# Graph network with four residual layers, one core: two rows per block on GpSimd, attention's closing steps moved behind the next block's masked scores, and the layer steps placed 8 groups later

## The chip, the cores and the metric

The kernel runs on one core of one Trainium2 chip. The metric is device time in microseconds (us). The core's engines are TensorE (PE in the profile; PEld is its weight load), VectorE (DVE), ScalarE (ACT), GpSimd (POOL) and SyncE (SP, which issues all DMAs here). They run side by side and wait for each other only at semaphores that the kernel writes out.

## The reference, cut to what matters

```python
x = LN(x + graph_conv(x, adj, L0_W, L0_b))      # layer 0: D^-1/2 (A+I) D^-1/2 x W^T + b
x = LN(x + attention(x, adj, WQ, WK, p))        # layer 1
x = LN(x + graph_conv(x, adj, L2_W, L2_b))      # layer 2
x = LN(x + graph_conv(x, adj, L3_W, L3_b))      # layer 3: D^-1/2 A D^-1/2 x W + b
# attention, for x of 8 x 2048 x 128, adj of 8 x 2048 x 2048:
q = x @ WQ;  k = x @ WK
h = relu(q[:, None, :, :] + k[:, :, None, :])   # 8 x 2048 x 2048 x 128
score = einsum('bijd,d->bij', h, p)
att = softmax(score + where(adj > 0, 0, -1e22)) ; out = att @ x
```

The tensor `h` is never stored. For each pair of sample and node i ("a row") the kernel makes a 128 x 2048 tile (feature by j) and TensorE contracts it with p at once.

## The kernel before, in words

**Blocks, groups, rows.** A sample has 16 blocks of 128 nodes, 128 blocks in all. A block has 32 groups (`g` 0 to 31) of 4 rows (`u` 0 to 3); "(1,3)" is row 3 of group 1. Twelve groups are of kind A (2, 5, 7, 10, 13, 15, 18, 21, 23, 26, 29, 31): ScalarE makes their rows, L861. The 20 others are of kind D: VectorE makes them as `max(q, -k)` on pairs of fp16, L1110. TensorE takes the groups in order, L1269. Each kind has a ring of 2 groups: the rows of a D group may only be made when TensorE has finished the D group before the last one (semaphore `rows_used["D"]`). Group 3 uses the slot of group 0, group 6 that of group 3, and so on.

**The order is written out by hand.** Each engine walks over `place = t*32 + g` and does at a place whatever the tables at the top of `build` put there, before or between the rows of that group. "Place 28" below is the group before whose rows the work stands.

**Masked scores.** The scores of block n are read out of PSUM inside block n+1 at (1,1): `masked_scores` (L1048, L1052). Its four bank reads wait for TensorE's last groups of block n (`bank_scored`, `rows_used`), and TensorE's group 0 of block n+1 waits bank by bank for them (`scores_read`). ScalarE takes the exponentials at place 5, TensorE turns them and multiplies by x at places 6 to 23, and VectorE ends the attention of block n at place 27 (`norm_inputs`: L1056, L1060, L1063, L1066: division by the row sum, residual, statistics) and place 30 (`att_out`, L1070). POOL computes the inverse root in between (`att_root`, L668, L670).

**Rows on other engines.** POOL makes row (1,3) of nearly every block (`row`, L679); it waits for the first bank of masked scores to be read. In 84 blocks it also makes row (30,3) (`sum_row`, L691), while VectorE does a layer step's sum; in the same number of cases VectorE makes a row of kind A (L1090).

**Layer steps beside the attention.** While attention runs on one sample, layers 2 and 3 of the sample before it and layer 0 of the one after it run in 12 steps of 512 nodes: layer 2 from blocks 2 to 5, layer 3 from 6 to 9, layer 0 from 10 to 13. A step adds 16 adjacency pieces (`add_piece`, L1183, at `PIECES_AT`), the self loop (`add_self`, L1189), is copied by ScalarE (`turn_layer`, L793), projected (`project`, L1201), summed with statistics by VectorE (`sum_layer`, L976, L984, L990) and normalised (`norm_layer`, L997); its bias is `add_bias`, L966. Layer 0 is followed by the new queries and keys (`QK`; L1213 and `split`, L1010, L1016). The first sample has no layers 2 and 3, the last has no layer 0. In blocks 0 to 9 also the next sample's adjacency is turned (`turn_unit`, places 0, 6, 10, 14, 18, 23, 28) and summed on ScalarE.

## Time and profile before

| | us |
|---|---|
| median of 3 runs | 13880.72 (13879.03 to 13884.08) |
| profiled execution, span | 13883.0 (no other time of it is given; it lies within the runs) |
| busy in it: DVE / PE / ACT / POOL | 13327.1 / 12956.7 / 12942.7 / 1095.3 |
| granted TensorE clock, mean | 0.989 |

The span runs from the first to the last instruction. Some 188 us at the start (first sample's adjacency) and 177 us after the last masked scores have no attention rows beside them; between them lie 127 intervals of 98 to 109 us, one per block. Idle time counts only where the engine is waited for afterwards, so what matters is the stretch of a block in which each engine waits.

### The profile page before, as it was taken

The numbers are of one execution on the slowest core, as the hardware profiler recorded it, in microseconds if no ns is written. First come the engines' busy times: TensorE is split into PE (matmuls) and PEld (weight loads), VectorE is DVE, ScalarE is ACT, GpSimd is POOL, SyncE is SP. The second block draws the span as 40 slices with busy tenths as digits, with TensorE's granted clock in tenths as the row PEclk, the third lists the DMA queues.
The fourth block names the chain that finished last, engine by engine and source line by source line (L and its number), as shares of the span: only waits on it lengthen the run. The fifth ranks groups of instructions, "written<-read, shape, count | busy, mean of one in ns | idle before, by whom it ended". The sixth has DMA issues, their size and how long they took to land.

```text
span 13883.0 us, 318102 instructions
## 1 busy us (share of the span) xinstructions
PE 12956.7 (93%) x143877; PEld 5442.7 (39%) x143877; DVE 13327.1 (96%) x14041; ACT 12942.7 (93%) x8528; POOL 1095.3 (8%) x706
## 2 busy tenths in 40 slices
PE   7889989999899999999999998999989999899988
PEld 3333434443344333444334443344434444333333
DVE  7999999999999999999999999999999999999995
ACT  6999999999999999999999999999999999999994
POOL 0000000010000100010000100001100010000000
PEclk9999999999999999999999999999999999999999
DMA  4111112221122112221122211222112221011103
GB/s 144 52 46 49 50 58 84 89 63 44 61 90 90 59 37 74 86 87 56 44 72 86 84 59 37 77 87 84 59 36 82 84 80 58 32 49 52 43 12 111
DMA packets 680284, 918.70 MB, mean 66 GB/s; under 512 B 60432, under 2 KB 421904, under 8 KB 659472
## 3 DMA queue, kind: packets, MB, share of 16 engines
q1 hardware_dynamic: 678928, 898.35, 20.7%
q8 instruction: 1129, 18.50, 0.6%
q14 instruction: 227, 1.86, 0.0%
HBM read 705.23 MB, written 184.55 MB: 64 GB/s over the span
## 4 chain that ended last, share of the span: by engine, by line
DVE 56%; PE 34%; ACT 7%; issue 2%; DMA 1%; POOL 0%; SPq 0%; DVEq 0%; POOLq 0%; ACTq 0%
DVE big L1110 50%; PE score L1269 24%; ACT big L861 6%; PE acc L1183 5%; PE acc L1242 2%; PE turn L1154 2%; DVE att L1048 2%; DVE big L1090 1%; DVE gx L997 1%; DMA piece<-adj_turned 0%; DVE gx L976 0%; PE turn L1213 0%; DVE stats L984 0%; ACT q_pair L769 0%; DVE att L1037 0%
## 5 line engine op out<-in xcount | busy, mean ns | idle before, releaser
L1110 DVE TENSOR_SCALAR big<-q_pair,k_pair_cols 128x2048 f32<-128x2048 f32 x10029 | 12094.2, 1278 | 289.8 <-PE score L1269 272.4
L861 ACT ACTIVATE big<-q_f,k_cols 128x2048 f32<-128x2048 f32 x6060 | 11633.5, 1998 | 256.9 <-PE score L1269 247.5
L1269 PE MATMUL score<-big,unit_window 128*32 128x512 f16 x82592 | 5439.0, 394 | 750.3 <-DVE big L1110 716.7
L1269 PE MATMUL score<-big,sign_window 128*32 128x512 f32 x48480 | 5591.5, 595 | 69.2 <-ACT big L861 67.5
L1269 PEld LDWEIGHTS score<-big,unit_window 128*32 128x32 bf16 x82592 | 2308.1, 96 | 3952.0 <-DVE big L1110 1128.8
L1269 PEld LDWEIGHTS score<-big,sign_window 128*32 128x32 f32 x48480 | 1572.3, 110 | 3299.2 <-issue 2948.4
L1183 PE MATMUL acc<-piece,q_f 128*128 128x512 f32 x2944 | 1411.5, 602 | 18.1 <-DVE q_f L959 10.7
L668 POOL TENSOR_SCALAR att_var<-att_mom 128x1 f32<-128x1 f32 x128 | 73.4, 573 | 9809.0 <-DVE att_mom L1066 9809.0
L1183 PEld LDWEIGHTS acc<-piece,q_f 128*128 128x128 f32 x2944 | 503.1, 190 | 529.8 <-issue 470.2
L1242 PE MATMUL acc<-x,att_turned 128*128 128x128 f32 x4096 | 559.4, 280 | 0.0
L1242 PEld LDWEIGHTS acc<-x,att_turned 128*128 128x128 f32 x4096 | 504.1, 194 | 56.8 <-issue 56.8
L837 ACT ACTIVATE att_turned<-turn 128x512 f32<-128x512 f32 x512 | 299.6, 585 | 160.1 <-PE turn L1154 160.0
L769 ACT ACTIVATE q_pair<-turn 128x512 f32<-128x512 f32 x448 | 261.4, 584 | 146.7 <-PE turn L1154 146.6
L679 POOL TENSOR_SCALAR big<-q_pair,k_pair_cols 128x2048 f32<-128x2048 f32 x127 | 250.5, 1973 | 1436.5 <-DVE bank_max L1048 1436.5
L1154 PEld LDWEIGHTS turn<-ident,att 128*128 128x128 f32 x2048 | 220.3, 143 | 340.8 <-issue 335.8
L1154 PE MATMUL turn<-ident,att 128*128 128x128 f32 x2048 | 343.6, 291 | 3.8 <-ACT att L833 3.1
L1048 DVE CUSTOM_DVE_ANT_0 att<-score,att 128x512 f32<-128x512 f32 x512 | 323.1, 684 | 10.4 <-PE score L1269 10.3
L1154 PE MATMUL turn<-ident,q_pair 128*128 128x128 f32 x1920 | 296.7, 279 | 27.3 <-DMA q_pair<-in_adj_dram 20.3
L833 ACT ACTIVATE att<-att,neg_max 128x2048 f32<-128x2048 f32 x128 | 256.1, 2000 | 51.5 <-DVE neg_max L1052 51.5
L1154 PEld LDWEIGHTS turn<-ident,q_pair 128*128 128x128 f32 x1920 | 219.6, 142 | 122.8 <-issue 92.9
L691 POOL TENSOR_SCALAR big<-q_pair,k_pair_cols 128x2048 f32<-128x2048 f32 x84 | 165.6, 1971 | 1110.2 <-DVE gx L976 1110.2
L782 ACT ACTIVATE y_turned<-q_pair 128x1024 bf16<-128x1024 f32 x224 | 237.1, 1059 | 7.1
(95 smaller groups left out, 2876.3 us busy)
## 6 DMA issues: line engine op xcount, KB each, us to landing
piece<-adj_turned SPq DMA_DIRECT2D x1472, 256.0 KB, 2.7
att<-in_adj_dram SPq DMA_DIRECT2D x128, 1024.0 KB, 5.2
q_pair<-in_adj_dram SPq DMA_DIRECT2D x240, 512.0 KB, 4.5
adj_turned<-q_pair SPq DMA_DIRECT2D x224, 512.0 KB, 4.8
adj_turned<-big SPq DMA_DIRECT2D x16, 1024.0 KB, 13.5
q_f<-in_adj_dram SPq DMA_DIRECT2D x16, 512.0 KB, 5.4
gx<-in_x_dram SPq DMA_DIRECT2D x32, 256.0 KB, 4.0
q_kept<-q_pair SPq DMA_DIRECT2D x32, 256.0 KB, 3.7
```

The costliest lines, as they stand in the source:

```text
L679: pool.tensor_scalar(ring["D"][:, RANK[g] % RING * 4 + u, :], pairs_of(c + 1), 3.0e38, k_pair_cols[:, t % 2, QUAD * u + g:QUAD * u + g + 1 ...
L769: nc.scalar.activation(stage(c)[:, k * BANK:(k + 1) * BANK], turn[1][:], ACT.Copy).then_inc(turn_free[1], 1)
L782: nc.scalar.activation(unread, raw(c), ACT.Abs, accum_out=abs_part[:, u % 2, u // 2:u // 2 + 1]).then_inc(raw_abs_summed, 1)
L833: nc.scalar.activation(att[:], att[:], ACT.Exp, bias=neg_max[:], accum_out=row_sum[:]).then_inc(exp_ready, 1)
L837: nc.scalar.activation(att_turned[:, cc % 2, :], turn[0][:], ACT.Copy).then_inc(turn_free[0], 1)
L861: ins = nc.scalar.activation(ring["A"][:, RANK[g] % RING * 4 + u, :], q_of(c + 1), ACT.Relu, bias=k_cols[:, t % 2, QUAD * u + g:QUAD * u + ...
L1048: nc.vector.tensor_tensor_reduce(out=part, in0=score[:, cc, :], in1=part, scale=1.0, scalar=-3.0e38, op0=ALU.add, op1=ALU.max, accum_out=b ...
L1110: ins = nc.vector.tensor_scalar(ring["D"][:, RANK[g] % RING * 4 + u, :], pairs_of(c + 1), k_pair_cols[:, t % 2, QUAD * u + g:QUAD * u + g ...
L1154: ins = nc.tensor.transpose(turn[k][:, j * P:(j + 1) * P], src(j), ident[:])
L1183: nc.tensor.matmul(acc[1][:], scaled(c)[:, i, :], turned, start=(i == 0), stop=(i == T - 1)) \
L1242: ins = nc.tensor.matmul(acc[0][:, 0:D], att_turned[:, cc % 2, j * P:(j + 1) * P], x1[:, cc * PER + j, :], start=(cc == 0 and j == 0), sto ...
L1269: ins = nc.tensor.matmul(score[QUAD * u:QUAD * (u + 1), cc, :], (unit_window if pair else sign_window)[:, QUAD - 1 - g:2 * QUAD - 1 - g], ...
```

## The change

POOL makes (3,3) as well as (1,3), both right after VectorE has made row (1,0) (new semaphore `window_open`). `norm_inputs` of block n goes from place 27 of block n+1 to right behind the masked scores in block n+2, `att_out` to place 6 there; `row_sum` gets two columns since the next exponentials come before it is read. All layer steps start 8 groups later (`STEP_SHIFT`), and the tables within a step are set anew.

```diff
+    BLOCK, STEP_SHIFT = {"layer2": 2, "layer3": 6, "layer0": 10}, 8
-    PIECES_AT = {-4: [0, 1, 2], 0: [3, 4, 5], 1: [6], 4: [7], 10: [8, 9], 14: [10], 18: [11], 23: [12, 13, 14, 15]}
-    SELF_AT, TURNED_AT, PROJECT_AT, SUM_AT, ROOT_AT, NORM_OUT_AT, STORE_AT = 18, 28, 28, 31, 33, 40, 41
+    PIECES_AT = {-4: [0, 1], 0: [2], 2: [3], 6: [4], 10: [5], 15: [6, 7, 8], 20: [9, 10, 11], 24: [12, 13, 14], 25: [15]}
+    SELF_AT, TURNED_AT, PROJECT_AT, SUM_AT, ROOT_AT, NORM_OUT_AT, STORE_AT = 15, 28, 28, 31, 33, 37, 38
...
-    QK = {"turn": 46, "copy": 49, "q": 50, "q_out": 54, "k": 55, "q_store": 56, "q_split": 58, "k_out": 59,
+    QK = {"turn": 47, "copy": 50, "q": 52, "q_out": 55, "k": 56, "q_store": 57, "q_split": 59, "k_out": 60,
...
+        row_sum = sb("row_sum", [P, 2])
...
-        MASK_AT, EXP_AT, NORM_AT, OUTPUT_AT = 24, 5, 27, 30
+        MASK_AT, EXP_AT, OUTPUT_AT = 24, 5, 6
-        POOL_ROW = (1, 3)
+        POOL_ROWS = [(1, 3), (3, 3)]
-        SUM_ROW = (30, 3)
+        SUM_ROW = ((SUM_AT + STEP_SHIFT - 1) % GROUPS, 3)
...
         def start_of(name, s):
-            return (BLOCK[name] + s) * GROUPS
+            return (BLOCK[name] + s) * GROUPS + STEP_SHIFT
...
-            def row(c, t):
-                g, u = POOL_ROW
+            def row(c, t, g, u):
                 n = block_of(c, t)
-                pool.wait_ge(scores_read, block_of(c, t) * CHUNKS + 1)
+                pool.wait_ge(window_open, n)
...
                 pool.wait_ge(rows_used["D"], n * N_OF["D"] + (RANK[g] + 1))
...
-                    if g == POOL_ROW[0] and has_pool_row(c, t):
-                        row(c, t)
+                    if g == POOL_ROWS[0][0] and has_pool_row(c, t):
+                        for at in POOL_ROWS:
+                            row(c, t, *at)
+                        if has_norm(c, t):
+                            att_root(block_of(c, t) - 2)
...
-                    if before and g == NORM_AT:
-                        norm_inputs(c * T + (T + t - 1), c + 1 if t > 0 else c, (t - 1) % T)
-                    if before and g == OUTPUT_AT:
-                        att_out(c * T + (T + t - 1), (t - 1) % T)
+                    if has_norm(c, t) and g == OUTPUT_AT:
+                        att_out(n - 2)
...
                             if before and u > 0 and (g, u) == masked_at(t):
                                 masked_scores(n)
+                                if has_norm(c, t):
+                                    norm_inputs(n - 2)
-                            if (g, u) == POOL_ROW and has_pool_row(c, t):
+                            if (g, u) in POOL_ROWS and has_pool_row(c, t):
                                 continue
...
+                            if before and (g, u + 1) == masked_at(t):
+                                ins.then_inc(window_open, 1)
```

Modulo 32, the pieces stood at places 28, 0, 1, 4, 10, 14, 18, 23 (3, 3, 1, 1, 2, 1, 1, 4 of them) and now stand at 28, 0, 1, 4, 8, 10, 14, 18, 23 (3, 3, 1, 2, 1, 1, 1, 1, 3). Projection goes from place 28 to 4 of the next block, the sum from 31 to 7, the normalisation from 8 to 13, the bias from 20 to 28, the self loop from 18 to 23.

VectorE, in a block in which layer 3 runs, before: from the statistics of the attention (`att_mom`) over a layer step's sum (L976 to L990) and the masked scores to the step's normalisation (L997).

```order
L1066 BN_AGGR att_mom<-att_stats 128x2
L1110 TENSOR_SCALAR big<-q_pair,k_pair_cols 128x2048 x8
L1070 TENSOR_SCALAR att_pre<-att_pre,att_mom,att_rstd 128x128
L1110 TENSOR_SCALAR big<-q_pair,k_pair_cols 128x2048 x3
L976 SCALAR_TENSOR_TENSOR gx<-acc,dis_use,gx 128x128 x4
L984 BN_STATS stats<-gx 128x6 x4
L990 BN_AGGR moments<-stats 128x2 x4
L1110 TENSOR_SCALAR big<-q_pair,k_pair_cols 128x2048 x5
```

The same engine in the same block now, from the last masked read on.

```order
L1062 TENSOR_REDUCE neg_max<-bank_max 128x1
L1067 RECIPROCAL row_inv<-row_sum 128x1
L1071 SCALAR_TENSOR_TENSOR att_pre<-acc,row_inv,x 128x128
L1074 BN_STATS att_stats<-att_pre 128x6
L1077 BN_AGGR att_mom<-att_stats 128x2
L1120 TENSOR_SCALAR big<-q_pair,k_pair_cols 128x2048 x9
L1082 TENSOR_SCALAR att_pre<-att_pre,att_mom,att_rstd 128x128
L1120 TENSOR_SCALAR big<-q_pair,k_pair_cols 128x2048 x3
L986 SCALAR_TENSOR_TENSOR gx<-acc,dis_use,gx 128x128 x4
L994 BN_STATS stats<-gx 128x6 x4
L1000 BN_AGGR moments<-stats 128x2 x4
L1120 TENSOR_SCALAR big<-q_pair,k_pair_cols 128x2048 x16
```

Attention's statistics and the step's sum stood before the masked scores and stand behind them; of the 14 rows that VectorE made from (1,1) to the end of group 6 it makes 12, the other two being POOL's (3,3) and (6,3), the row beside the sum.

TensorE at places 28 and 4, before: first place 28 with the projection (L1201) and three pieces, then place 4 with one piece.

```order
L1154 MATMUL turn<-ident,q_pair 128x128 x4
L1201 MATMUL acc<-w_layer,y_turned 128x128 x4
L1183 MATMUL acc<-piece,q_f_0 128x512 x3
L1269 MATMUL score<-big,unit_window 32x512 x32
...
L1183 MATMUL acc<-piece,q_f_0 128x512
L1269 MATMUL score<-big,unit_window 32x512 x32
L1269 MATMUL score<-big,sign_window 32x512 x16
```

TensorE at the same two places now.

```order
L1167 MATMUL turn<-ident,q_pair 128x128 x4
L1196 MATMUL acc<-piece,q_f_0 128x512 x3
L1282 MATMUL score<-big,unit_window 32x512 x32
...
L1214 MATMUL acc<-w_layer,y_turned 128x128 x4
L1196 MATMUL acc<-piece,q_f_0 128x512 x2
L1282 MATMUL score<-big,unit_window 32x512 x32
L1282 MATMUL score<-big,sign_window 32x512 x16
```

The projection has left place 28 and stands at place 4, with one more piece behind it.

## Rows read from the trace of the kernel before

**Rows 1.** The page: busy us (share of span) by engine; the chain by engine

```profile
PE 12956.7 (93%) x143877; PEld 5442.7 (39%) x143877; DVE 13327.1 (96%) x14041; ACT 12942.7 (93%) x8528; POOL 1095.3 (8%) x706
DVE 56%; PE 34%; ACT 7%; issue 2%; DMA 1%; POOL 0%; SPq 0%; DVEq 0%; POOLq 0%; ACTq 0%
```

**Rows 2.** Waits over the span: us in total, times, longest

```profile
PE score L1269 <- DVE big L1110: 716.7, 577, 2.8
DVE big L1110 <- PE score L1269: 272.4, 305, 2.7
```

**Rows 3.** Windows from masked score to masked score: blocks 0, 7, 12; PE, PEld, DVE, ACT, POOL

```profile
5258.34:5361.49 103.15, 91.84 (x1103) 38.12 (x1102) 101.83 (x98) 100.01 (x74) 5.41 (x3) 0.98 0.17 54
6003.53:6110.54 107.01, 103.76 (x1141) 44.32 (x1142) 103.63 (x113) 105.04 (x75) 8.34 (x6) 1.00 0.32 96
6538.54:6645.62 107.08, 103.70 (x1129) 43.13 (x1128) 104.69 (x116) 99.05 (x61) 9.91 (x6) 1.00 0.21 62
```

**Rows 4.** Timeline, DVE, blocks 6 to 7: start, us, what, [idle before]

```profile
5979.47 0.15 DVE L1056 RECIPROCAL row_inv<-row_sum 128x1 f32<-128x1 f32 x1
...
5980.38 0.18 DVE L1066 BATCH_NORM_AGGREGATE att_mom<-att_stats 128x2 f32<-128x6 f32 x1
5981.78 9.65 DVE L1110 TENSOR_SCALAR big<-q_pair,k_pair_cols 128x2048 f32<-128x2048 f32 x8 [1.22 <-PE score L1269]
...
5995.19 1.12 DVE L976 SCALAR_TENSOR_TENSOR gx<-acc,dis_use,gx 128x128 f32<-128x128 f32 x4
...
5997.55 6.04 DVE L1110 TENSOR_SCALAR big<-q_pair,k_pair_cols 128x2048 f32<-128x2048 f32 x5
6003.51 0.68 DVE L1048 CUSTOM_DVE_ANT_0 att<-score,att 128x512 f32<-128x512 f32 x1
...
6006.14 16.93 DVE L1110 TENSOR_SCALAR big<-q_pair,k_pair_cols 128x2048 f32<-128x2048 f32 x14
6022.98 1.11 DVE L997 TENSOR_SCALAR gx<-gx,moments,rstd 128x128 f32<-128x128 f32 x4
...
6044.80 2.48 DVE L1110 TENSOR_SCALAR big<-q_pair,k_pair_cols 128x2048 f32<-128x2048 f32 x2 [1.56 <-PE score L1269]
```

**Rows 5.** Timeline, PE, block 7: groups 31, 0 and 9

```profile
6000.72 2.76 PE L1269 MATMUL score<-big,sign_window 128*32 128x512 f32 x24
...
6006.57 2.00 PE L1269 MATMUL score<-big,unit_window 128*32 128x512 f16 x32
...
6033.72 2.01 PE L1269 MATMUL score<-big,unit_window 128*32 128x512 f16 x32 [1.73 <-DVE big L1110]
```

**Rows 6.** Timeline, PE, block 0: group 0

```profile
5259.16 2.38 PE L1269 MATMUL score<-big,unit_window 128*32 128x512 f16 x32 [0.43 <-DVE bank_max L1048]
```

**Rows 7.** Timeline, POOL: a row and a small operation, block 7; two small ones elsewhere

```profile
6004.30 1.97 POOL L679 TENSOR_SCALAR big<-q_pair,k_pair_cols 128x2048 f32<-128x2048 f32 x1 [6.68 <-DVE bank_max L1048]
6006.23 1.27 POOL L662 TENSOR_SCALAR var_eps<-moments 128x4 f32<-128x4 f32 x1
...
4710.19 0.23 POOL L668 TENSOR_SCALAR att_var<-att_mom 128x1 f32<-128x1 f32 x1 [76.86 <-DVE att_mom L1066]
...
6239.47 11.93 POOL L704 TENSOR_TENSOR dis_new<-deg_sum,minus_half 128x16 f32<-128x16 f32 x3 [15.31 <-DVE deg_sum L942]
```

**Rows 8.** Timeline, DVE beside the last of rows 7

```profile
6239.31 14.44 DVE L1110 TENSOR_SCALAR big<-q_pair,k_pair_cols 128x2048 f32<-128x2048 f32 x12
```

**Rows 9.** Groups by line: shape xcount | busy us, mean ns | idle before

```profile
L1183 PE MATMUL acc<-piece,q_f 128*128 128x512 f32 x2944 | 1411.5, 602 | 18.1 <-DVE q_f L959 10.7 <-DMA piece<-adj_turned 6.3
...
L1201 PE MATMUL acc<-w_layer,y_turned 128*128 128x128 f32 x768 | 106.9, 282 | 8.9 <-ACT y_turned L793 8.9
...
L966 DVE TENSOR_TENSOR gx<-gx,bias_layer 128x512 f32<-128x512 f32 x96 | 65.5, 682 | 0.1
```

**Rows 10.** Timeline, ACT, block 7: exponentials; the wait at place 13

```profile
6007.84 1.99 ACT L833 ACTIVATE att<-att,neg_max 128x2048 f32<-128x2048 f32 x1
...
6037.68 0.60 ACT L769 ACTIVATE q_pair<-turn 128x512 f32<-128x512 f32 x1 [1.81 <-PE turn L1154]
```

More of the change, by code:

```diff
@@ L273, in pool_rows, with pool_rows_before, has_norm @@
         def pool_rows(c, t):
-            return max(c * T + (T + t - 1), 0)
-        SUM_ROW = (30, 3)
+            return max(c * T + (T + t - 1), 0) * len(POOL_ROWS)
+        def pool_rows_before(g):
+            return sum(h < g for h, _ in POOL_ROWS)
+        def has_norm(c, t):
+            return block_of(c, t) > 1
+        SUM_ROW = ((SUM_AT + STEP_SHIFT - 1) % GROUPS, 3)
         def sums_at(c, t):
-            return steps_at(c, t * GROUPS + SUM_AT, SUM_AT)
+            return steps_at(c, t * GROUPS + SUM_ROW[0] + 1, SUM_AT)
         def has_sum_row(c, t):
@@ L294, in lent_rows @@
                 return []
-            return LENT_ROWS[:1 if steps_at(c, t * GROUPS + SELF_AT, SELF_AT) else 2]
+            return LENT_ROWS[:1 if steps_at(c, t * GROUPS + STEP_SHIFT, 0) else 2]
         def lent_before(c, t, g):
@@ L617, in attention @@
                             load_q(c + 1)
-                    if before and g == OUTPUT_AT + 1:
-                        store_x2(c * T + (T + t - 1), (t - 1) % 2)
+                    if block_of(c, t) > 1 and g == OUTPUT_AT + 1:
+                        store_x2(block_of(c, t) - 2, t % 2)
             sp.dma_start(diag[:], diagonals[0], allow_slow_non_contiguous=True).then_inc(diag_loaded, 16)
@@ L642, in _ @@
             attention(LAST)
-            store_x2(B * T - 1, 1)
+            for m in (B * T - 2, B * T - 1):
+                store_x2(m, m % 2)
             for place in range(PLACES):
@@ L737, in _ @@
             attention(LAST)
-            att_root(B * T - 1)
+            for m in (B * T - 2, B * T - 1):
+                att_root(m)
             for place in range(PLACES):
@@ L832, in exponentials @@
                 act.wait_ge(neg_max_ready, n)
-                nc.scalar.activation(att[:], att[:], ACT.Exp, bias=neg_max[:], accum_out=row_sum[:]).then_inc(exp_ready, 1)
+                nc.scalar.activation(att[:], att[:], ACT.Exp, bias=neg_max[:],
+                                 accum_out=row_sum[:, (n - 1) % 2:(n - 1) % 2 + 1]).then_inc(exp_ready, 1)
             def copy_weights(m, cc):
@@ L1066, in norm_inputs, with att_out @@
                 nc.vector.bn_aggr(att_mom[:], att_stats[:]).then_inc(att_moments_ready, 1)
-            def att_out(m, t):
+            def att_out(m):
+                t = m % T
                 dve.wait_ge(att_rstd_ready, m + 1)
@@ L1084, in attention @@
                     side(c, place)
-                    if before and (g, 0) == masked_at(t):
-                        masked_scores(n)
                     for h, u in lent_rows(c, t):
@@ L1123, in _ @@
             masked_scores(B * T)
-            norm_inputs(B * T - 1, B - 1, T - 1)
-            att_out(B * T - 1, T - 1)
+            for m in (B * T - 2, B * T - 1):
+                norm_inputs(m)
+                att_out(m)
             for place in range(PLACES):
@@ L1248, in score_rows @@
                 kind, n = KIND[g], block_of(c, t)
-                if g == POOL_ROW[0] and has_pool_row(c, t):
-                    pe.wait_ge(pool_row_ready, pool_rows(c, t) + 1)
+                if g in [h for h, _ in POOL_ROWS] and has_pool_row(c, t):
+                    pe.wait_ge(pool_row_ready, pool_rows(c, t) + pool_rows_before(g) + 1)
                 if g == SUM_ROW[0] and has_sum_row(c, t):
```

16 lines of the change are left out of this document (7 added, 9 removed).

## The prediction

> **What bounds the kernel now.** Read the page first: three engines are busy for 93 to 96% of the span, and the chain goes through VectorE for 56% and TensorE for 34% [rows 1]. No engine bounds it alone. The waits say the same: TensorE waits 716.7 us for VectorE's rows, VectorE 272.4 us for TensorE [rows 2]. So it matters where in a block each wait falls, and the windows show that this depends on the kind of block [rows 3]. In block 0, without a layer step, VectorE is busy 101.83 of 103.15 us and TensorE 91.84: VectorE bounds it. In block 7, with a step, idle are TensorE 3.2 us, VectorE 3.4 and ScalarE 2.0; in block 12 3.4, 2.4 and 8.
>
> The timeline of block 7 gives the places. M is the start of its masked scores (6003.51). VectorE waits 1.22 us for TensorE ahead of place 27 (5981.78), then not until place 14, where it waits 1.56 (6044.80) [rows 4]. TensorE waits 1.73 us ahead of group 9 (6033.72) [rows 5]. Hence VectorE's work from place 27 to group 9 is the bound, then TensorE's from group 9 to 11, and after a second such change (VectorE to place 20, TensorE to group 24) it begins again. Work taken out of the right piece shortens the block; work put beside it is free until it has filled the other engine's wait.
>
> **The units.** A VectorE row takes 14.44 / 12 = 1.20 us [rows 8]. An adjacency piece is two records, 1411.5 / 1472 = 0.96 us, the projection 106.9 / 96 = 1.1, the bias 0.68 [rows 9]. Attention's statistics take 5979.47 to 5980.56 and some 0.1 to the next row, 1.2 us; a step's sum with its statistics 5995.19 to 5997.55, 2.4; its normalisation 6022.98 to 6024, 1.0; the masked reads 6003.51 to 6006.14, 2.6 [rows 4].
>
> **POOL's second row.** It takes 1.20 us off VectorE in 127 blocks. But it needs slot 0 of the ring, so it starts only when TensorE is through with group 0: in block 7 at 6008.57, M + 5.1 [rows 5], in block 0 at 5261.54, 3.2 us after its M of 5258.34 [rows 3, 6]. VectorE's stretch with no row in it is now the masked reads and the statistics, M to M + 3.8. So in block 0 POOL's row of 1.97 us [rows 7] overhangs the stretch by 1.4 us, and in block 7 it begins among VectorE's rows.
>
> What does that cost VectorE? No row of before shows a long POOL operation beside its rows. Short ones show one direction: 0.23 us for att_var while VectorE has no row running, but 1.27 for L662, begun as a row began and ended as it ended [rows 4, 7]. The three L704 took 11.93 us beside twelve rows that kept their 1.20 [rows 7, 8]. POOL waits for the end of a row and is then let in. For the other direction the bounds are 0 (those twelve lost nothing) and 1.97 (the whole row) plus a row's wait, 3.2. I take exclusion both ways: 1.97, less the 0.13 by which VectorE's next row began before POOL's end (6006.14 against 6006.27) [rows 4, 7], less the 0.2 that a POOL operation lasts with hardly any data: 1.6 us among rows, and 3.2 + 1.97 - 0.13 - 3.8 = 1.25 in blocks like 0.
>
> The Trainium skill speaks against the change here: "SBUF — State Buffer", section on the two separate sides, has GpSimd and a VectorE operation in a 2-port mode share one port pair as an exclusive lock for the whole instruction, the loser fully blocked. The short operations agree with it on POOL's side; no row here shows VectorE's. Taken to the letter it would make the 1.6 a full 1.97, some 30 us more over the 77 blocks with steps if nothing else absorbed it.
>
> The 44 blocks without a step (12 in the first sample, 4 in each of six, 8 in the last): -1.20 + 1.25, +2 us in all.
>
> **The moves, in a block like 7.** Ahead of M VectorE loses statistics, att_out and sum (1.2 + 0.3 + 2.4) and gets bias and row (30,3) (0.7 + 1.2): 2.0 less. The masked reads also need TensorE's group 31, which ended at M [rows 5] and now ends 1.1 earlier without the projection. Only the last of four reads needs its end, and that read begins 1.8 us after the first, so VectorE can use the 2.0: M' = M - 2.0. Behind M' VectorE gets 1.2 + 0.3 + 2.4, loses normalisation, (3,3) and (6,3) (1.0 + 1.2 + 1.2), +0.5, and 1.6 for POOL: its rows of group 9 are ready at -2.0 + 0.5 + 1.6 = +0.1. TensorE comes 1.1 earlier and gets projection and a piece each at places 4 and 8, 3.0 us, against its waits of 1.73 and (by difference to its idle time, with 1.1 at group 20) some 0.4: -0.2. So group 9 comes at +0.1 by VectorE and at -0.2 by TensorE, and POOL's 1.6 us hide almost wholly beside TensorE's new work; if that cover were gone they would cost 1.6. From there: place 10 a piece less, -0.9 for TensorE; VectorE's normalisation stands at place 13 in its wait of 1.56; place 20 the bias less, -1.6; place 23 a piece less, -2.5.
>
> ScalarE caps that. Its idle time is 2.0, of it 1.81 at place 13 [rows 3, 10]. It also gets a new wait at place 4: its copy of the step needs the last piece, which stands at TensorE's place 1, ended at M + 5.1 + 0.96 before and 1.1 earlier now. The exponentials began at M + 4.3 [rows 10] and come after it and a copy: about 1.2 us later, within the 1.81. The cap is some 1.8; with three engines this near to each other I take -1.6 for the 28 blocks of layer 3: -45.
>
> In layer 2 (21 blocks) the self loop's products (four, as the projection's, 1.1) go from place 18 to 23 and eat the piece gone there: -1.5, -32. In layer 0 (28 blocks) ScalarE has 8 us of room, TensorE and VectorE 3.4 and 2.4 of idle time [rows 3]; two pieces and, in three blocks of four, the products for q and k leave the stretch behind group 9 that TensorE bounds, while the first q split (1.2 us of VectorE) comes behind M. Limits: 2.4 less 0.4 (POOL's 1.6 less the row's 1.2), 2.0; I take -1.7, -47. Block 2 gets its first pieces later and block 14 a step's end: the same work elsewhere, 0. The start and the end have no rows beside them, 0.
>
> **Sum.** +2 - 45 - 32 - 47 = -122 on 13883.0, which is 2.3 above the median of the runs: 13,760.
>
> **Rivals.**
> *POOL's row costs VectorE nothing.* For it the twelve undisturbed rows [rows 8], against it 1.27 for 0.23 [rows 7]. Blocks without a step then give 1.2 (-53), layers 2 and 3 about their caps (-36, -50), layer 0 2.4 (-67): -206, 13,675.
> *ScalarE and TensorE take it back.* The new wait at place 4 and the 3.0 us moved behind M each just exceed their room (1.81 and 2.1 + 1.1), since a late group delays all that share the rings. Layers 2 and 3 stand still, layer 0 gives 0.7: -18, 13,865.
> *Slower: POOL is kept out until VectorE pauses.* VectorE's rows follow each other without a gap [rows 8]. If POOL's long row is let in only at a pause, that is when VectorE has made three rows of group 3 and four of group 4 and must wait for TensorE's group 3, which waits for POOL: M' + 6.2 + 3.6 + 4.8 = 14.6, POOL ends at M' + 16.6, TensorE's group 3 at M + 16.6 instead of 12.4. TensorE has no wait left to take it in: +4.2 - 1.6 in 77 blocks, +200: 14,080. It decides once POOL waits over 2 us behind TensorE's group 0. Against it: the short operations got in at the first row's end.
>
> **Chances.** Forecast 0.52 (its own range 13,710 to 13,840), POOL free 0.15, taken back 0.18, kept out 0.15. A measurement of this kernel can tell 0.2%, 28 us. Faster: 0.46 + 0.15 + 0.05 = 0.66. Same: 0.04 + 0.10 = 0.14. Slower, with milder forms of the last case: 0.02 + 0.03 + 0.15 = 0.20. The range of 8 in 10 takes in most of the free case and all between the forecast and the third, and leaves the full price of the last out: 13,670 to 13,930.
>
> **What would show it.** POOL's second row ends about 2 us behind TensorE's group 0, at M + 5.2 in blocks like 0, and one VectorE row behind it is longer or later by 1.2 to 1.6 us. Blocks like 0 keep their 103 us, blocks like 7 go to 105.4. TensorE's wait ahead of group 9 is under 0.5 us; ScalarE waits at place 4 and no longer at 13. Wrong would be: blocks like 0 at 102 (POOL free), POOL's row late by over 2 us (kept out), or blocks like 7 still at 107 with ScalarE idle at place 4.

## The result and the profile after

| | before | changed |
|---|---|---|
| median of 6 runs, us | 13884.45 (13879.03 to 13890.18) | 13926.18 (13915.42 to 13930.77) |
| profiled execution, span, us | 13883.0 | 13925.6 |
| granted TensorE clock, mean | 0.989 | 0.988 |

The ratio is 1.0029, with an interval of 1.0017 to 1.004: slower by 42 us, where 122 faster was forecast. The range held the time, the direction was wrong.

The page of the changed kernel: busy us (share of span), the chain by engine, and the two groups of rows.

```profile
PE 13003.6 (93%) x143877; PEld 5453.8 (39%) x143877; DVE 13372.5 (96%) x13914; ACT 12936.6 (93%) x8528; POOL 1624.1 (12%) x833
...
DVE 67%; PE 24%; ACT 6%; issue 2%; DMA 1%; POOL 0%; SPq 0%; DVEq 0%; POOLq 0%; ACTq 0%
...
L1120 DVE TENSOR_SCALAR big<-q_pair,k_pair_cols 128x2048 f32<-128x2048 f32 x9902 | 12081.4, 1295 | 276.4 <-PE score L1282 264.6
...
L686 POOL TENSOR_SCALAR big<-q_pair,k_pair_cols 128x2048 f32<-128x2048 f32 x254 | 655.4, 2580 | 11105.3 <-DVE big L1120 10743.0
```

Against [rows 1] VectorE has 127 instructions fewer and is busy 45 us longer, and the chain goes through it for 67% instead of 56%. 127 rows of 1.20 us were taken from it, and their time came back: the mean of a row is 1295 ns (1278 before), that of a POOL row 2580 (1.97 us in [rows 7]). Where the 17 ns come from stands in the spread of durations. One line's instructions in the changed kernel, min/median/max in ns, VectorE and then POOL:

```profile
L1120 DVE TENSOR_SCALAR big<-q_pair,k_pair_cols x9902: 1251/1280/2998, 188.9 to 13730.4; 128x2048 f32<-128x2048 f32 x199
...
L686 POOL TENSOR_SCALAR big<-q_pair,k_pair_cols x254: 1969/1979/4174, 294.7 to 13639.8; 128x2048 f32<-128x2048 f32 x127
```

The median has not moved. Before, the longest of VectorE's 10029 rows took 1307 ns; now 93 take 2.8 to 3.0 us. POOL's second row takes up to 4.17. The other 34 of the 127 blocks have no long row; there another VectorE operation is stretched, for example the split of new queries (822 ns at most before):

```profile
L1026 DVE TENSOR_TENSOR q_pair<-q_pair x64: 729/778/2453, 113.6 to 12026.6; 128x512 f16<-128x512 f32 x64
```

Of these operations 21 are on L1026, 7 on L1020 and 6 on L969. The 127 stretched operations together are 208 us longer than the median of their kind, 1.64 us each, and the 127 rows taken away were worth 152: the busy time that came back is more than was saved.

The waits over the span, us in total, times, longest:

```profile
PE score L1282 <- DVE big L1120: 649.2, 562, 4.6
...
DVE big L1120 <- PE score L1282: 264.6, 254, 2.3
...
ACT y_turned L802 <- PE acc L1196: 395.3, 90, 32.1
```

TensorE's longest wait for VectorE has gone from 2.8 us [rows 2] to 4.6, and ScalarE's copy of a step's sum waits 90 times where it waited 12 times (192.3 us) before.

The windows of blocks 0, 7 and 12, to be laid beside [rows 3] (PE, PEld, DVE, ACT, POOL, granted clock):

```profile
5275.84:5379.80 103.96, 91.70 (x1112) 38.37 (x1108) 102.48 (x97) 100.68 (x75) 7.70 (x4) 0.98 0.14 44
6029.07:6135.48 106.41, 104.25 (x1144) 44.05 (x1140) 103.87 (x112) 104.20 (x74) 14.42 (x7) 1.00 0.32 97
6558.26:6665.50 107.24, 104.69 (x1132) 42.98 (x1128) 104.81 (x114) 98.59 (x61) 12.44 (x7) 1.00 0.21 62
```

Block 0 was to stay at 103.15 and takes 103.96; block 7 was to go to 105.4 and takes 106.41; block 12 was to lose 1.7 and takes 0.16 more. The same over all blocks: means over five samples of the time from one M to the next, in us, summed over the blocks named (M as in the prediction, read from the trace's semaphore events):

| blocks | before | changed | shift alone (first experiment) |
|---|---|---|---|
| 0, 1, 14, 15 | 411.9 | 418.5 | 415.8 |
| 2 | 108.5 | 109.4 | 106.3 |
| 3 to 5 | 322.3 | 322.0 | 318.8 |
| 6 | 106.9 | 109.0 | 108.6 |
| 7 to 9 | 322.4 | 318.8 | 314.8 |
| 10 to 13 | 427.9 | 426.1 | 424.0 |
| sample | 1699.9 | 1703.8 | 1688.4 |

**Block 7, engine by engine.** POOL, start, us, what, [idle before]; M is now 6029.07:

```profile
6029.23 1.97 POOL L686 TENSOR_SCALAR big<-q_pair,k_pair_cols 128x2048 f32<-128x2048 f32 x1 [81.37 <-DVE big L1120]
6034.46 3.62 POOL L686 TENSOR_SCALAR big<-q_pair,k_pair_cols 128x2048 f32<-128x2048 f32 x1 [3.25 <-PE score L1282]
6038.05 1.19 POOL L676 TENSOR_SCALAR att_var<-att_mom 128x1 f32<-128x1 f32 x1
```

The first row lies beside the masked reads and takes its 1.97 us. The second starts at M + 5.4, when TensorE has done group 0, and takes 3.62: about 1.65 of waiting, then its own 1.97. VectorE at the same time and before it:

```profile
6008.10 4.87 DVE L1120 TENSOR_SCALAR big<-q_pair,k_pair_cols 128x2048 f32<-128x2048 f32 x4 [1.38 <-PE score L1282]
6012.90 0.68 DVE L976 TENSOR_TENSOR gx<-gx,bias_layer 128x512 f32<-128x512 f32 x1
6013.50 15.63 DVE L1120 TENSOR_SCALAR big<-q_pair,k_pair_cols 128x2048 f32<-128x2048 f32 x13
6029.05 0.68 DVE L1058 CUSTOM_DVE_ANT_0 att<-score,att 128x512 f32<-128x512 f32 x1
...
6031.68 0.15 DVE L1067 RECIPROCAL row_inv<-row_sum 128x1 f32<-128x1 f32 x1
...
6032.68 12.46 DVE L1120 TENSOR_SCALAR big<-q_pair,k_pair_cols 128x2048 f32<-128x2048 f32 x9
```

Two things are to be seen. Nine rows took 12.46 us where 9 x 1.20 = 10.8 are needed: the exclusion of POOL and VectorE (the "lock" from here on) costs VectorE 1.66. No semaphore stands behind this wait, so what the opening says, that engines wait for each other only at semaphores, does not hold for these two. And the wait of 1.22 us at place 27 [rows 4] is still there, now 1.38: from its end to M pass 6029.05 - 6008.10 = 20.95 us, before 6003.51 - 5981.78 = 21.73. M has come nearer by 0.8 us, not by 2.0. TensorE ahead of group 9 and at places 10 to 13:

```profile
6060.94 2.00 PE L1282 MATMUL score<-big,unit_window 128*32 128x512 f16 x32 [0.85 <-DVE big L1120]
6062.88 0.66 PE L1167 MATMUL turn<-ident,att 128*128 128x128 f32 x4
6063.37 1.06 PE L1255 MATMUL acc<-x,att_turned 128*128 128x128 f32 x8
6064.26 0.60 PE L1167 MATMUL turn<-ident,q_pair 128*128 128x128 f32 x4
6064.70 1.02 PE L1196 MATMUL acc<-piece,q_f 128*128 128x512 f32 x2
...
6073.62 2.78 PE L1282 MATMUL score<-big,sign_window 128*32 128x512 f32 x24 [0.67 <-ACT big L871]
```

The wait ahead of group 9 was to be under 0.5 us and is 0.85, and VectorE is what it waits for. ScalarE's copy of the step at place 4, and its copy of the turned unit at place 10:

```profile
6035.42 0.60 ACT L802 ACTIVATE y_turned<-acc 128x512 f32<-128x512 f32 x1 [1.15 <-PE acc L1196]
6035.91 1.99 ACT L842 ACTIVATE att<-att,neg_max 128x2048 f32<-128x2048 f32 x1
...
6064.90 0.60 ACT L778 ACTIVATE q_pair<-turn 128x512 f32<-128x512 f32 x1 [0.96 <-PE turn L1167]
```

The first wait is there as foreseen, 1.15 us. The second was to vanish from 1.81 us [rows 10]; 0.96 are left, and TensorE pays 0.67 for them three places on.

### The profile page after: what moved, and what is told of

It is laid out like the page before. It is cut to its first block, busy times and chain, and to the rows that moved or that the text cites. A ratio compares the mean times of both kernels' runs of the same rounds, so it can differ in the third digit from the quotient of the medians.

```text
span 13925.6 us, 318482 instructions
## 1 busy us (share of the span) xinstructions
PE 13003.6 (93%) x143877; PEld 5453.8 (39%) x143877; DVE 13372.5 (96%) x13914; ACT 12936.6 (93%) x8528; POOL 1624.1 (12%) x833
## 4 chain that ended last, share of the span: by engine, by line
DVE 67%; PE 24%; ACT 6%; issue 2%; DMA 1%; POOL 0%; SPq 0%; DVEq 0%; POOLq 0%; ACTq 0%
DVE big L1120 60%; PE score L1282 17%; ACT big L871 5%; PE acc L1196 3%; DVE att L1058 2%; PE acc L1255 2%; PE turn L1167 1%; DVE big L1098 1%; DVE gx L986 1%; DVE q_pair L1026 1%; DMA piece<-adj_turned 1%; DVE stats L994 0%; PE acc L1202 0%; DVE q_f L969 0%; DVE gx L1007 0%
## 5 line engine op out<-in xcount | busy, mean ns | idle before, releaser
L1120 DVE TENSOR_SCALAR big<-q_pair,k_pair_cols 128x2048 f32<-128x2048 f32 x9902 | 12081.4, 1295 | 276.4 <-PE score L1282 264.6
L686 POOL TENSOR_SCALAR big<-q_pair,k_pair_cols 128x2048 f32<-128x2048 f32 x254 | 655.4, 2580 | 11105.3 <-DVE big L1120 10743.0
L802 ACT ACTIVATE y_turned<-acc 128x512 f32<-128x512 f32 x96 | 57.5, 599 | 395.3 <-PE acc L1196 395.3
L1058 DVE CUSTOM_DVE_ANT_0 att<-score,att 128x512 f32<-128x512 f32 x512 | 323.4, 686 | 13.4 <-PE score L1282 13.2
L678 POOL TENSOR_TENSOR att_rstd<-att_var,minus_half 128x1 f32<-128x1 f32 x128 | 283.3, 2213 | 10.7
L698 POOL TENSOR_SCALAR big<-q_pair,k_pair_cols 128x2048 f32<-128x2048 f32 x84 | 165.6, 1971 | 740.5 <-DVE gx L986 740.5
```

The costliest lines, as they stand in the source:

```text
L678: pool.tensor_tensor(att_rstd[:], att_var[:], minus_half[:, 0:1], ALU.pow).then_inc(att_rstd_ready, 1)
L686: pool.tensor_scalar(ring["D"][:, RANK[g] % RING * 4 + u, :], pairs_of(c + 1), 3.0e38, k_pair_cols[:, t % 2, QUAD * u + g:QUAD * u + g + 1 ...
L1058: nc.vector.tensor_tensor_reduce(out=part, in0=score[:, cc, :], in1=part, scale=1.0, scalar=-3.0e38, op0=ALU.add, op1=ALU.max, accum_out=b ...
L1120: ins = nc.vector.tensor_scalar(ring["D"][:, RANK[g] % RING * 4 + u, :], pairs_of(c + 1), k_pair_cols[:, t % 2, QUAD * u + g:QUAD * u + g ...
```

## The experiments

Eleven kernels ran, each beside the kernel before, whose medians in these four sessions lay between 13,882.6 and 13,884.5; differences of 10 us and more between kernels are read below, together with the ranges of the table. The edits are shown against the changed kernel unless another is named, and cut to what matters. All medians in us; the expectations say themselves what each theory held.

| run | median (range, runs) | ratio to before, 95% |
|---|---|---|
| e1_shift_only | 13794.33 (13791.54 to 13798.84, 5) | 0.9936, 0.9924 to 0.9949 |
| e2_one_row | 13835.55 (13831.55 to 13838.20, 6) | 0.9965, 0.9953 to 0.9978 |
| e3_stats_back | 13819.27 (13814.73 to 13823.54, 5) | 0.9954, 0.9942 to 0.9967 |
| e4_rows_in_group1 | 13775.98 (13772.60 to 13778.20, 5) | 0.9923, 0.9910 to 0.9935 |
| e5_row_left_out | 13765.07 (13760.02 to 13766.00, 4) | 0.9914, 0.9900 to 0.9927 |
| e6_group1_stats_back | 13804.08 (13798.12 to 13805.41, 5) | 0.9942, 0.9929 to 0.9954 |
| e7_units_first | 13734.41 (13733.98 to 13737.13, 4) | 0.9892, 0.9877 to 0.9907 |
| e8_turn_after_exp | 13711.92 (13709.74 to 13713.95, 4) | 0.9875, 0.9861 to 0.9888 |
| e9_before_units_first | 13856.56 (13850.84 to 13861.77, 11) | 0.9980, 0.9971 to 0.9989 |
| e10_before_two_rows | 13955.76 (13950.47 to 13958.47, 5) | 1.0050, 1.0038 to 1.0063 |
| e11_third_row | 13805.75 (13802.85 to 13809.38, 5) | 0.9944, 0.9930 to 0.9957 |

### The three parts apart

**e1_shift_only**: the steps 8 groups later with their tables, one POOL row, the statistics where they were.

```diff
-        POOL_ROWS = [(1, 3), (3, 3)]
+        POOL_ROWS = [(1, 3)]
-        MASK_AT, EXP_AT, OUTPUT_AT = 24, 5, 6
+        MASK_AT, EXP_AT, NORM_AT, OUTPUT_AT = 24, 5, 27, 30
...
+                    if has_norm(c, t) and g == NORM_AT:
+                        norm_inputs(n - 1)
...
```

> The layer steps' shift and their new tables alone: POOL makes one row, attention's statistics are back at place 27 of the next block. Theory S (shadow: the statistics cost nothing at place 27, in front of VectorE's wait of 1.2 us, and cost 1.2 us behind the masked scores; the second row costs 1.6 and saves 1.2; the shift itself gains): 13,800 to 13,840, below the kernel before (13,884). Theory L (layers: the shift costs, by ScalarE's new wait at place 4, by scaling and other work that now falls behind the masked scores): 13,900 to 13,940, as slow as the changed kernel.

Measured 13,794, 90 us faster than before and 6 below the range of the theory that held. Block 7 takes 105.36 us, which is what the forecast gave to the whole change. VectorE, start, us, what, [idle before]:

```profile
5947.68 0.16 DVE L1065 RECIPROCAL row_inv<-row_sum 128x1 f32<-128x1 f32 x1
...
5948.58 0.18 DVE L1075 BATCH_NORM_AGGREGATE att_mom<-att_stats 128x2 f32<-128x6 f32 x1
5949.13 4.90 DVE L1118 TENSOR_SCALAR big<-q_pair,k_pair_cols 128x2048 f32<-128x2048 f32 x4 [0.36 <-PE score L1279]
```

With the statistics at place 27 the wait behind them is 0.36 us; without them it is 1.38 in the changed kernel. They stand in the shadow of that wait. (Their output, `att_out`, is back at place 30 in this kernel too.)

**e2_one_row**: the changed kernel with POOL's (1,3) alone.

```diff
-        POOL_ROWS = [(1, 3), (3, 3)]
+        POOL_ROWS = [(1, 3)]
```

> The changed kernel with POOL making (1,3) only; shift and moved statistics stay. Theory S: the second row saves 1.2 us and costs 1.6 to 1.7, so without it 0.4 to 0.5 us less per block where VectorE bounds it and little elsewhere: 13,870 to 13,900. If the second row was of use (POOL's lock costs nothing or hides), this is slower than the changed kernel's 13,926, by up to 150 us. Theory L: 13,915 to 13,930.

Measured 13,836, below every case. So the moved statistics cost 41 us (e2 less e1) and the second row another 91.

**e3_stats_back**: the changed kernel, both rows, statistics at place 27 (the second half of e1's edit).

```diff
-        MASK_AT, EXP_AT, OUTPUT_AT = 24, 5, 6
+        MASK_AT, EXP_AT, NORM_AT, OUTPUT_AT = 24, 5, 27, 30
...
```

> The changed kernel with two POOL rows and the shift, but attention's statistics back at place 27 (and their output at 30) of the next block. Theory S: 1.2 us less per step block, so 13,926 less 60 to 90, 13,835 to 13,865; blocks without a step get no shorter, since VectorE's free stretch ends 1.2 us earlier and POOL's second row begins among its rows either way. Theory L: 13,915 to 13,940.

Measured 13,819, again below what was expected. The second row costs 25 us here (e3 less e1) against 91 behind the moved statistics. The parts do not add up, and this asked for a cause of its own (e11 below).

### The lock

**e4_rows_in_group1**: both rows begin in the stretch in which VectorE makes none; their slot is free before the masked scores, so the second need not wait for TensorE's group 0.

```diff
-        POOL_ROWS = [(1, 3), (3, 3)]
+        POOL_ROWS = [(1, 2), (1, 3)]
-                    pe.wait_ge(pool_row_ready, pool_rows(c, t) + pool_rows_before(g) + 1)
+                    pe.wait_ge(pool_row_ready, pool_rows(c, t) + pool_rows_before(g + 1))
```

> The changed kernel with POOL's two rows as (1,2) and (1,3): their ring slot is free before the masked scores, so the second row need not wait for TensorE's group 0. It then runs from M + 2.1 to M + 4.1 and overhangs VectorE's free stretch (to M + 3.6) by some 0.4 us. Theory S: 1.2 saved for 0.4, against 1.2 for 1.7 now: 1.3 us less per block where VectorE bounds, about 1 elsewhere: 13,780 to 13,830. If it is not the lock that ate the row's gain, 13,910 to 13,930.

Measured 13,776, 150 us below the changed kernel by moving one row, and 4 below the range. The durations of POOL's and VectorE's rows in this kernel, min/median/max in ns:

```profile
L686 POOL TENSOR_SCALAR big<-q_pair,k_pair_cols x254: 1959/1971/2016, 297.1 to 13495.3; 128x2048 f32<-128x2048 f32 x127
...
L1120 DVE TENSOR_SCALAR big<-q_pair,k_pair_cols x9902: 1249/1281/2600, 191.2 to 13585.0; 128x2048 f32<-128x2048 f32 x199
```

POOL is never kept waiting (2016 at most, against 4174). A little of the lock is left on VectorE, whose longest row takes 2.6 us: some 120 rows are stretched, by 35 us in all.

**e5_row_left_out**:

```diff
                     if g == POOL_ROWS[0][0] and has_pool_row(c, t):
-                        for at in POOL_ROWS:
-                            row(c, t, *at)
+                        row(c, t, *POOL_ROWS[0])
...
-                if g in [h for h, _ in POOL_ROWS] and has_pool_row(c, t):
+                if g == POOL_ROWS[0][0] and has_pool_row(c, t):
```

This kernel leaves the row out: no engine makes (3,3), and TensorE no longer waits for it.

> The changed kernel with row (3,3) left out: neither POOL nor VectorE makes it, so TensorE contracts an old row there. This is what the second row would give if POOL made it at no cost to anyone. Against the changed kernel (13,926) it prices POOL's row, against the kernel with one POOL row (13,836) VectorE's. Theory S: VectorE's row 1.2 us in 127 blocks, about two thirds of it on the path, 90 to 140 us below 13,836: 13,700 to 13,745; so POOL's row costs 180 to 225 us, 1.4 to 1.8 per block. If what costs is not the long POOL operation but the wait of TensorE's group 3 or the order of the instructions, the gap to 13,836 is as large, but blocks without a step show no VectorE row of 2.9 us and still more than 102 us.

Measured 13,765, 20 us above the range: VectorE's row is on the path for less than the two thirds expected. The run prices the row: made by VectorE it costs 70 us (e2 less e5, 0.56 a block), by POOL at (3,3) 161 (1.27 a block), by POOL in the open stretch 11 (e4 less e5). In the changed kernel the row costs more on the idle engine than on the busy one. TensorE's waiting for POOL's late row does not explain this: over the span of the changed kernel no wait of its matmuls is put down to the rows of L686.

**e10_before_two_rows**: POOL's second row added to the kernel before, nothing else.

```diff
-        POOL_ROW = (1, 3)
+        POOL_ROWS = [(1, 3), (3, 3)]
...
+                        for at in POOL_ROWS:
+                            row(c, t, *at)
```

> The kernel before with POOL's second row (3,3) alone, no shift, statistics at place 27. Lock theory: VectorE's free stretch ends at M + 2.6, before the row can begin (M + 3.2 to 5.1), so it always falls among VectorE's rows and costs 1.7 for 1.2: 0.5 us in each block where VectorE bounds and some in the others, 13,900 to 13,950. If the row's cost hides beside TensorE (as the prediction had it): 13,860 to 13,890.

Measured 13,956, 72 us slower than before and 6 above the range of the lock theory: the row hurts without any of the other edits. Here all 127 stretched operations are rows; they are 213 us longer, against 152 saved, and the difference of 61 is most of the 72.

### The statistics, and when the lock counts

**e6_group1_stats_back**: e4 with the statistics back at place 27, the edit of e3.

> Two POOL rows as (1,2) and (1,3) with the shift, and attention's statistics back at place 27. VectorE's free stretch ends at M + 2.6, the second row at M + 4.1: it overhangs by 1.4 us and saves 1.2. Theory S: no gain of the second row, but no statistics behind the masked scores: within 15 us of the shift alone (13,794). If a long POOL operation did not block VectorE, 60 to 100 us below it.

Measured 13,804, within 15 us of the shift alone as expected, and 28 above e4. POOL's second row again overhangs the stretch: 126 VectorE rows take 2.3 to 2.6 us, 161 us in all against the 152 saved. So the moved statistics cost 41 us beside one row at (1,3), 107 beside (3,3) (changed kernel less e3), and gain 28 beside two rows in group 1: there they also lengthen the stretch in which VectorE makes no row, and of the 161 us of lock only 35 are left (e4).

Much of this comes out of one pair of numbers: when VectorE has the rows of group 9 ready, and when TensorE has done group 9, which takes it 2.0 us if it waited. Means over the 80 blocks of five samples, us after M, from the semaphore events:

| kernel | VectorE ready | TensorE done | median, us |
|---|---|---|---|
| before | 30.19 | 32.45 | 13884 |
| e10: before, (3,3) by POOL | 30.76 | 33.07 | 13956 |
| e1: shift | 30.74 | 33.20 | 13794 |
| e3: shift, (3,3) | 31.13 | 33.32 | 13819 |
| e2: shift, statistics | 31.86 | 34.09 | 13836 |
| changed: shift, statistics, (3,3) | 32.43 | 34.72 | 13926 |
| e6: shift, two rows in group 1 | 30.80 | 33.26 | 13804 |
| e4: e6 and statistics | 31.15 | 33.57 | 13776 |
| e11: e4 and (3,3) | 31.55 | 33.79 | 13806 |

The lock makes VectorE 0.4 to 0.6 us late in each pair (1.6 less the row's 1.2). TensorE follows by 0.12 where it ended last itself (e1, e3) and by 0.63 where it was waiting already (e2, changed). That is the cover of the prediction, and the statistics had used it up: they make VectorE 1.1 us late at group 9. Against this they bring M nearer. From the three pairs: TensorE done later by 0.89, 1.40 and 0.31, time of the kernel +41, +107 and -28 us over 127 blocks, or +0.32, +0.84 and -0.22 a block; the difference is 0.57, 0.56 and 0.53. So taken from ahead of M the statistics and their output are worth some 0.55 us, not 1.2 or more.

The 0.55 is a mean of two kinds of block. From the same events, the time from TensorE's end of group 9 to the next M falls by 1.2 to 1.3 us on average in blocks 0, 1, 14 and 15, and by 0.3 to 0.4 in blocks 2 to 13 (by 0.26 in block 7, in e2 against e1). The 0.3 is about what `att_out` takes (0.33 us), which stood at place 30, behind the wait at place 27. So in a block like 7 the statistics themselves gave next to nothing.

**What the table leaves.** Beside the moved statistics the second row costs 91 us, and the 0.4 of the lock, 1.64 less 1.20, makes only 56 over 127 blocks. The means of the blocks in the same five samples show where the rest lies: with the row, blocks 3, 4, 5, 7, 8, 10 and 11 take 0.4 us longer each, but blocks 1, 2 and 9 take 1.6, 2.4 and 1.5 longer, over half of the 10 us of a sample. Why these three pay more is open. Over the whole run TensorE's granted clock is at its lower level for 113 us in these blocks in the changed kernel, and for 55 in e2. By an estimate from these numbers that takes up to 29 us more of TensorE's time, and no run separates it from the lock.

**e11_third_row** tests this where its answer was not known: (3,3) added to e4.

```diff
-        POOL_ROWS = [(1, 3), (3, 3)]
+        POOL_ROWS = [(1, 2), (1, 3), (3, 3)]
```

> Changed kernel with three rows by POOL: (1,2) and (1,3) in the stretch in which VectorE makes none, as in the run with both rows in group 1, and (3,3) behind TensorE's group 0, as in the changed kernel. It asks when the lock on (3,3) costs time. Cover: the lock makes VectorE's rows of group 9 later by 0.4 us (1.6 less the 1.2 of the row), and that counts only where VectorE ends last at group 9. With both rows in group 1 VectorE is ready for group 9 at M + 31.15 on average (mean of 80 blocks) and TensorE has done group 9 at M + 33.57, 2.4 us later, where 2.0 to 2.2 is the mark of TensorE having waited: so there are 0.2 to 0.4 us of room, and the row costs 0 to 0.2 us a block, 0 to 25 us: 13,770 to 13,805. Own price: the row at (3,3) costs its 72 to 91 us wherever it is added (row alone on before, and behind the moved statistics): 13,848 to 13,867. In block 7 by the first TensorE does not wait ahead of group 9, by the second it does, by some 0.4 us or more.

Measured 13,806, 30 us over e4: 1 us beyond the end of the range of the one theory, 42 below that of the other. TensorE in block 7 at groups 8 and 9, in e1, e3, e2 and e11 in turn:

```profile
5999.09 3.83 PE L1279 MATMUL score<-big,unit_window 128*32 128x512 f16 x64
```

```profile
6012.09 3.94 PE L1279 MATMUL score<-big,unit_window 128*32 128x512 f16 x64
```

```profile
6024.75 1.99 PE L1282 MATMUL score<-big,unit_window 128*32 128x512 f16 x32
6027.14 2.01 PE L1282 MATMUL score<-big,unit_window 128*32 128x512 f16 x32 [0.39 <-DVE big L1120]
```

```profile
6009.81 2.00 PE L1282 MATMUL score<-big,unit_window 128*32 128x512 f16 x32
6012.07 2.01 PE L1282 MATMUL score<-big,unit_window 128*32 128x512 f16 x32 [0.26 <-DVE big L1120]
```

With the statistics at place 27 the two groups run into each other (x64), without the second row (e1) and with it (e3). With the statistics alone TensorE waits 0.39 us, with both 0.85 (above). In e4 the groups run together as well, and in e11 the lock uses up that room and shows 0.26 us of wait: neither none, as the cover theory had it for block 7, nor the 0.4 or more of the other.

### The gain that stayed away behind group 9

**e7_units_first**: e4, with the turns of the next sample's adjacency (`turn_units`) ahead of attention's turn and product at places 10, 14, 18 and 23, since ScalarE's rows of group 13 stand behind its copy of the turn of place 10.

```diff
-            def side(c, place):
+            def turn_units(c, place):
                 for k in range(2):
                     for u in units_where(c, lambda u: slot_place(2 * u + k) == place):
                         turn_unit(c, u, k)
+
+            def side(c, place):
...
+                    turn_units(c, place)
                     if before and g in TURN_AT:
```

> The fastest so far (rows (1,2) and (1,3), 13,776) with TensorE's turns of the next sample's adjacency ahead of attention's turn and product at places 10, 14, 18, 23 instead of behind. Theory S13: ScalarE's rows of group 13 stand behind its copy of the turn of place 10, and TensorE waits for them in blocks 0 to 9, so a piece taken from behind that turn at place 10 gave nothing; turning 1.7 us earlier should give 0.5 to 1 us in some 70 blocks: 13,710 to 13,745. If the place-10 chain does not bound: 13,765 to 13,785, or slower, since attention's own copies come 0.6 us later.

Measured 13,734, as expected 42 us below e4. The waits, us in total, times, longest:

```profile
PE score L1284 <- ACT big L871: 128.6, 138, 2.6
```

It was 150.2 us, 154 times, in e4. The total came as expected, but not where it was expected: in the mean of five samples blocks 0, 1, 6 and 14 are 1.0, 1.2, 1.0 and 0.8 us shorter, and the blocks 3 to 5, 7 and 8, in which the chain through place 10 was to bound, by 0.15 at most.

**e8_turn_after_exp**: e7, with ScalarE's copy of a step's sum (and the projection) a place later, behind the exponentials.

```diff
-    SELF_AT, TURNED_AT, PROJECT_AT, SUM_AT, ROOT_AT, NORM_OUT_AT, STORE_AT = 15, 28, 28, 31, 33, 37, 38
+    SELF_AT, TURNED_AT, PROJECT_AT, SUM_AT, ROOT_AT, NORM_OUT_AT, STORE_AT = 15, 29, 29, 31, 33, 37, 38
```

> The fastest so far (13,734) with ScalarE's copy of a step and TensorE's projection one place later, at 5 and not 4: the copy then stands behind the exponentials, which need not wait for TensorE's last piece. Theory: in step blocks ScalarE from its wait at place 4 (1.1 us) to its rows of group 13, for which TensorE waits 0.7 us, is the chain that is left; 0.4 to 0.7 us less in 49 blocks of layers 2 and 3: 13,700 to 13,715. If VectorE or TensorE alone bounds these blocks: 13,725 to 13,745.

Measured 13,712, in the range, 22 us below e7, the fastest of all and 172 us below the kernel before. The waits again:

```profile
ACT y_turned L802 <- PE acc L1196: 253.0, 54, 32.0
...
PE score L1284 <- ACT big L871: 73.5, 86, 2.6
```

The copy waits 54 times instead of 90, and TensorE's waits for ScalarE's rows fall from 128.6 to 73.5 us: the wait at place 4 was paid for. Blocks 3 to 5, 7 and 8 are 0.3 to 0.6 us shorter; blocks 12 to 14, of which the theory said nothing, 1.0 to 1.1.

**e9_before_units_first**: e7's edit on the kernel before.

```diff
...
+                    turn_units(c, place)
                     if before and g in TURN_AT:
```

> The kernel before with one edit: the turns of the next sample's adjacency ahead of attention's turn and product at places 10, 14, 18 and 23. Theory S13 (ScalarE's rows of group 13 hang on the turn of place 10, and bound blocks 0 to 9 of the kernel before as well, VectorE's wait of 1.56 us at place 14 being their echo): 0.6 to 1.2 us less in some 70 blocks, 13,800 to 13,840. If that chain bounds only the changed kernels: 13,875 to 13,890.

Measured 13,857, 27 us faster: between the two ranges, so neither theory has it. The waits did fall: ScalarE's ahead of its copy of the turned unit from 146.6 to 83.8 us (from 84.1 to 54.9 in e7), and TensorE's for ScalarE's rows from 67.5 to 44.1 (from 150.2 to 128.6 in e7). Blocks 0, 1 and 2 are 1.2, 0.7 and 1.3 us shorter, blocks 3 to 8 by 0.2 at most. So the chain through place 10 bounds the step blocks of neither kernel.

## Why the prediction was wrong

**"Ahead of M VectorE 2.0 less ... M' = M - 2.0."** This step failed. VectorE's stretch starts at the end of its wait at place 27, and the statistics (1.2 us) stood ahead of that wait: [rows 4] have them at 5979.47 and the wait of 1.22 us behind them. TensorE's group 24 sets the wait's end, so only sum and att_out less bias and row count: 2.7 - 1.9 = 0.8, and 0.8 was measured in block 7. The prediction had read the wait and named it the start of the bound stretch (though "ahead of place 27", where it lies behind the statistics of that place), and then counted work on its far side. Behind M' the prediction charged them, with `att_out`, at 1.5 us; VectorE was 1.1 (e2 less e1) to 1.3 us (changed kernel less e3) later at group 9. Over all blocks the move ahead of M is worth 0.55 us, and 0.3 in blocks 2 to 13.

**"POOL's 1.6 us hide almost wholly beside TensorE's new work."** The size of the lock was right: 1.66 in the nine rows, 1.64 on average over the 127 stretched operations. The cover was real too (e3: 25 us in all, e11: 30). But it rested on M' - 2.0. With 0.8, VectorE is ready for group 9 at +1.3 by the prediction's own terms, +0.9 as measured, and not at +0.1, and TensorE's -0.2 no longer counts: TensorE was done with group 24 of the block before and then with group 9 54.9 us apart, before 54.0. The clause "if that cover were gone they would cost 1.6" was the case that came. Less the row's 1.2 it is the 0.4 us of most blocks. That makes 56 of the 91 us between e2 and the changed kernel; the rest lies mostly in blocks 1, 2 and 9, and its cause is open.

**"+2 in all" for blocks without a step.** The second row was to begin at M + 3.2 and so to overlap the stretch. In block 0 of the window above (M at 5275.84) TensorE got to group 0 late, behind group 31 and the turn of a unit, and POOL began at M + 4.4, among rows:

```profile
5280.24 2.30 POOL L686 TENSOR_SCALAR big<-q_pair,k_pair_cols 128x2048 f32<-128x2048 f32 x1 [2.26 <-PE score L1282]
```

```profile
5279.45 11.34 DVE L1120 TENSOR_SCALAR big<-q_pair,k_pair_cols 128x2048 f32<-128x2048 f32 x8
```

Eight rows take 11.34 us; eight undisturbed ones took 9.65 [rows 4]. On average TensorE was done with group 0 at M + 4.6 in blocks 0, 14 and 15, before at 3.3. Block 0 takes 1.0 us longer; e4, where both rows lie in the stretch, has it at 102.29 instead of 104.17.

**"Block 2 ... and block 14 ...: the same work elsewhere, 0."** The shift alone makes blocks 1, 6, 14 and 15 longer by 0.6, 1.7, 2.2 and 1.1 us and block 2 shorter by 2.2: 3.4 a sample, some 24 us in all. In block 6 layer 3's normalisation now stands at places 3, 5 and 7, in the stretch that VectorE bounds.

**"Place 10 a piece less, -0.9."** ScalarE's copy hangs on the unit turn, which stands ahead of the piece, so the missing piece did not make it earlier: its wait of 1.81 us is still 0.96. In a block like 7 this cost next to nothing, since e7, which turns the unit first, shortens block 7 by 0.06 us; its 42 us come from other blocks. **The new wait at place 4** was foreseen (1.15 us against an estimate of 1.2) and judged to lie within ScalarE's room; e8 puts its price at 22 us. This is the rival in which ScalarE and TensorE take the gain back, in a small part.

**What was right.** The gain of the shift behind group 9: from there to group 24 block 7 takes 51.5 us in the changed kernel and in e1, before 53.0. That e1's block 7 meets the forecast of 105.4 so closely is in part luck, since that figure was for the whole change; over a sample the shift gives 11.5 us, where some 18 were forecast for the change. The exclusion of POOL and VectorE was right, in both directions, with its size. The Trainium skill, "SBUF — State Buffer", the section on the two separate sides, calls it an exclusive lock for the whole instruction; the trace agrees (3.62 us for POOL's row, of it 1.65 waited; 1.66 added to VectorE's nine), with two corrections. VectorE loses 1.66 and not 1.97. And "for the whole instruction" does not hold for every one of POOL's: its three `tensor_tensor` operations, 11.93 us together, held up none of twelve rows [rows 7, 8].

**The rivals.** POOL free is refuted by the rows of up to 2998 ns and by e10. Kept out until VectorE pauses is refuted: the longest second row took 4.17 us, where that rival needs some 10. But POOL is not always let in at the end of the running row, as the prediction read from the short operations: ahead of 84 of the 93 long rows VectorE began one more row after POOL was ready, and in 24 blocks POOL waited over 2 us, the sign that the prediction gave to this rival. e1 shows, too, that ScalarE and TensorE do not take the gain of the moves back as a whole.

**Open.** The first sample is 12 us longer and the end behind the last M 6, where I had put 0. The first sample's 12 are the same parts again: the shift takes 11 off (e1), the moved statistics add 7 (e2), the second row 16; of the end's 6 the row adds 4. Why the row costs most in blocks 1, 2 and 9 is open, and so is why e7 and e9 gain in the blocks in which they do. What the clock (below) adds is open too: between the first and the last M it is at its lower level for 232 us before, 201 in e1, 150 in e2 and 256 in the changed kernel. By an estimate from these numbers that can be at most 12 of the 42 us between the kernel before and the changed one, but more between e2 and the changed one.

## What to carry to other kernels

Before work is moved off a bound engine, find the last wait on that engine ahead of it: work on the near side of a wait that another engine ends is already free, and moving it past the wait adds its whole duration to where it goes. Where an idle engine and the bound one exclude each other, place the idle engine's work in stretches in which the bound engine has no such instructions: in this kernel a row cost 11 us there and 161 outside. And when two edits lean on the same slack, time them alone and together; 25 and 41 us became 132.
